# Local-attention stack: sums of squares behind the rope products, seeds ahead of the copy of O, band mask as eight tiled matmuls

## The reference

```
q, k, v = split(shift_tokens(x) @ Wqkv)          # 16 heads of 64
q = q / max(|q|, 1e-12) * q_scale;  k likewise   # one norm per token and head
q = q*cos*scale + rotate_half(q)*sin*scale;  k with 1/scale
# windows of 32 queries; each sees its own and the previous window, 64 keys
sim = einsum(q, keys) * 8
sim = where((i < j) | (i > j + 32) | (j is before the sequence), -max, sim)
out = softmax(sim) @ values;   x = out @ Wo + x
```

## Time and profile before

| what | us |
|---|---|
| median of 3 runs | 4362.58 (4357.62 to 4364.63) |
| the profiled execution's own time | 4365.13 |
| its span | 4363.3 |
| PE busy / weight loads | 3866.2 / 2314.4 |
| DVE / ACT / POOL busy | 3296.5 / 2534.1 / 2498.8 |

### The profile page before, as it was taken

One profiled execution on the slowest core, in us unless ns is written; L12 is line 12 of the kernel. 1 busy time (PEld: TensorE's weight loads), 2 busy tenths in 40 slices (PEclk: granted clock), 3 DMA queues, 4 the chain that ended last, 5 costly groups with the idle time before them and its releaser, 6 DMA issues. The chain is left out here.

```text
span 4363.3 us, 151598 instructions
## 1 busy us (share of the span) xinstructions
PE 3866.2 (89%) x66488; PEld 2314.4 (53%) x66488; DVE 3296.5 (76%) x4385; ACT 2534.1 (58%) x3236; POOL 2498.8 (57%) x2036
## 2 busy tenths in 40 slices
PE   6887799999999999999778877899999999999997
PEld 3323456665665666665433334566666666666664
DVE  7997777888888787888454436788888878878884
ACT  6885456566665666666324444556566565666654
POOL 0001677777777777777100005786777777777773
PEclk8999999999999999999789998999999999999998
DMA  0001232332323233222000002323323223232221
GB/s 19 1 1 42 72 87 65 85 77 75 83 67 87 73 78 85 62 67 62 17 1 1 1 14 74 92 62 84 81 67 85 73 79 80 73 81 71 66 60 40
DMA packets 165593, 260.83 MB, mean 60 GB/s; under 512 B 58572, under 2 KB 79816, under 8 KB 164936
## 3 DMA queue, kind: packets, MB, share of 16 engines
q1 hardware_dynamic: 164936, 251.13, 22.2%
HBM read 48.61 MB, written 1.05 MB: 11 GB/s over the span
## 5 line engine op out<-in xcount | busy, mean ns | idle before, releaser
L1374 POOL TENSOR_TENSOR f_k_rotated<-f_rope_ak,f_rope_bk 128x1024 f32<-128x1024 f32 x192 | 454.5, 2367 | 288.7 <-DVE f_rope_bk L1429 288.7
L1097 PE MATMUL banks<-f_wqkv,H 128*128 128x512 f32 x1152 | 564.9, 614 | 17.4 <-DVE f_E L1469 9.2
L1097 PE MATMUL banks<-f_wqkv,G 128*128 128x512 f32 x1152 | 551.8, 601 | 0.0
L1426 DVE TENSOR_TENSOR f_rope_aq<-banks,f_rope 128x1024 f32<-128x1024 f32 x192 | 235.1, 1225 | 389.5 <-ACT f_sqq L1284 376.2
L1361 POOL MEMSET f_kT<- 128x256 f32 x2 | 0.6, 311 | 839.9 <-POOLq L514 460.5
L1374 POOL TENSOR_TENSOR f_q_rotated<-f_rope_aq,f_rope_bq 128x1024 f32<-128x1024 f32 x192 | 454.5, 2367 | 29.0 <-DVE f_rope_bq L1429 28.6
L1319 ACT ACTIVATE f_V<-banks 128x1024 f32<-128x1024 f32 x192 | 196.8, 1025 | 418.7 <-PE banks L1097 418.3
L1152 PEld LDWEIGHTS banks<-f_O_T,f_wo 128*128 128x128 f32 x3072 | 372.6, 192 | 98.3 <-issue 94.6
L1152 PE MATMUL banks<-f_O_T,f_wo 128*128 128x128 f32 x3072 | 375.4, 275 | 6.4 <-issue 5.2
L1392 POOL TENSOR_TENSOR f_E<-f_E,f_row_inverse 128x1024 f32<-128x1024 f32 x192 | 368.6, 1920 | 19.8 <-DVE f_row_inverse L1484 19.8
L1386 POOL TENSOR_TENSOR f_q_rotated<-f_q_rotated,f_inverse_norm 128x1024 f32<-128x1024 f32 x192 | 365.2, 1902 | 15.0
(11 more groups left out here) (207 smaller groups left out, 8961.6 us busy)
## 6 DMA issues: line engine op xcount, KB each, us to landing
f_P_T_paired<-f_P_T SPq DMA_DIRECT2D x1536, 64.0 KB
f_V_previous<-f_V SPq DMA_DIRECT2D x192, 384.0 KB, 3.7
f_V_previous<-f_V SPq DMA_DIRECT2D x192, 128.0 KB, 2.4
f_wqkv<-in_L_ffn_Wqkv SPq DMA_DIRECT2D x48, 384.0 KB, 4.1
f_rope<-in_rope SPq DMA_DIRECT2D x24, 512.0 KB, 5.1
f_wo<-in_L_ffn_Wo SPq DMA_DIRECT2D x12, 512.0 KB, 5.4
f_w<-in_L_ffn_W SPq DMA_DIRECT2D x12, 341.0 KB
f_w<-in_L_ffn_W SPq DMA_DIRECT2D x24, 64.0 KB
```

What stands on the lines that cost most here:

```text
L1097: mm = nc.tensor.matmul(ps[:, o * BLK:(o + 1) * BLK], xs, w[:, c * INNER + o * BLK:c * INNER + (o + 1) * BLK], start=True, stop=True)
L1374: nc.gpsimd.tensor_tensor(qk[i][:], ra[i][:], rb[i][:], ALU.add).then_inc(radd.sem, 1)
L1426: nc.vector.tensor_tensor(heads_of(ra[i][:]), src, table(2 * i, 0, DH), ALU.mult).then_inc(rot.sem, 1)
```

## The change

Three edits in the stack. On DVE the sum of squares of q follows directly behind the rope products of q, and the sum for k and the clamp directly behind those of k. On ACT the Ln and Exp of the seeds stand ahead of the copy of O. On PE the mask is written by eight matmuls of 64 rows and 32 columns, in the tiling of the score matmuls, in place of two of 128 by 128; for this the mask table has one more block of entries set.

```
@@ scores
-                for i in range(2):
-                    nc.tensor.matmul(PT_S[:, i * BLK:(i + 1) * BLK], ident16[:],
-                                     mask[:, (1 if t else 0):(2 if t else 1), :].to_broadcast([P, HP, 2 * W]),
-                                     start=True, stop=False)
+                for g in range(NG):
+                    v = 1 if t or g else 0
+                    for i in range(2):
+                        rows = slice(i * DH, (i + 1) * DH)
+                        nc.tensor.matmul(PT_S[g * W:(g + 1) * W, i * BLK:(i + 1) * BLK], ident16[rows, i * DH:i * DH + W],
+                                         mask[rows, v:v + 1, :].to_broadcast([DH, HP, 2 * W]), start=True, stop=False)
@@ scalar
+                if live(s):
+                    act.wait_ge(clamped.sem, clamped.at(n))
+                    act.wait_ge(newton.sem, newton.past(n - 1))
+                    nc.scalar.activation(lg[:], ss[n % 2][:], ACT.Ln).then_inc(seeded.sem, 1)
+                    act.wait_ge(seeded.sem, seeded.at(n, 1))
+                    nc.scalar.activation(y0[:], lg[:], ACT.Exp, scale=-0.5).then_inc(seeded.sem, 1)
                 if live(s - 3):
                     act.wait_ge(o_mm.sem, o_mm.at(n - 3))
...
-                if live(s):
-                    act.wait_ge(clamped.sem, clamped.at(n))
-                    act.wait_ge(newton.sem, newton.past(n - 1))
-                    nc.scalar.activation(lg[:], ss[n % 2][:], ACT.Ln).then_inc(seeded.sem, 1)
-                    act.wait_ge(seeded.sem, seeded.at(n, 1))
-                    nc.scalar.activation(y0[:], lg[:], ACT.Exp, scale=-0.5).then_inc(seeded.sem, 1)
@@ vector
                     rotate(s, 0, q_mm, PQ)
+                    sums(n, 0)
...
                     rotate(s, 1, k_mm, PK)
+                    sums(n, 1)
+                    dve.wait_ge(red.sem, red.at(n))
+                    nc.vector.tensor_scalar(ss[n % 2][:], ss[n % 2][:], 1e-24, None, ALU.max).then_inc(clamped.sem, 1)
...
-                if live(s):
-                    sums(n, 0)
-                    sums(n, 1)
-                    dve.wait_ge(red.sem, red.at(n))
-                    nc.vector.tensor_scalar(ss[n % 2][:], ss[n % 2][:], 1e-24, None, ALU.max).then_inc(clamped.sem, 1)
@@ constants
     band[0:W, 0, 0:W] = NEG
+    band[2 * W:3 * W, 0, 0:W] = NEG
```

## The result

The changed kernel takes 4792.62 us (median of 4 runs, 4787.78 to 4800.77) against 4363.6 before: a ratio of 1.0988 (1.0969 to 1.1007), 429 us slower. The forecast was 4396 with a range of 4352 to 4430. The sign was right, the size was wrong: 34 us forecast, 429 measured.

The account below looks back on a forecast made before the run. A ring of waits through k's normalisation, not PE, was taken to pace the slot; the change makes the subtraction's ring bind. 4365.1 + 49 - 15 = 4399, on the median 4396 us; range 4352 to 4430.

Parts of the forecast that it names:

- The ring through the norms: k transposes to normalised k, through DVE, ACT and POOL: paces the old slot, loses 3.5 us, no longer binds.
- the ring through the subtraction: From q's projection through DVE's subtraction to PE's wait and the next projection: binds at 17.46 us in most slots.
- The length of the new ring: 18.56 + 17.46 + 17.46 + 16.60 = 70.08 us per group against 68.96: +1.12, over 44 groups +49 us.
- The first slots, -15 us: Slots without feed-forward work: new ring 16.60 or less against 17.54 a slot, about -15 us over two calls.
- Sum k to clamp 1.24, clamp 0.09: DVE terms of the new ring, ahead of the maximum (1.25) and the subtraction (1.22), in us.
- The clock: Rival: PE's new idle time costs clock; called unlikely. Shares the much slower case's chance of 0.10 with serial masks.
- the 2.35 of the earlier trace: PE's idle time in us in an early slot, where granted clock was 0.89; new waits were expected shorter.
- The mask: Eight mask matmuls on PE: 0.38 us for 0.52, gain 0.14 a slot, invisible because PE waits anyway.
- the lower bound of 0.26: Mask matmuls on PE if all eight tiles run together as one stream: 0.26 us.
- 4.6: How many score matmuls run abreast in the same tiling; used to price the eight masks at 0.38 us.
- ACT: Seeds ahead of the copy of O: delay it at most about half a us, no effect on time.

Follow-up runs that it names:

- the late clamp: Changed kernel with the clamp moved behind the subtraction and the seeds in their old place on ACT: 4394.93 us, ratio 1.0071.
- the two runs with the clock up: Changed kernel without the clamp, 4381.76 us; changed kernel with three useless matmuls on PE ahead of the wait for the subtraction, 4633.25 us.
- the filled wait: Changed kernel with three useless 512-column matmuls on PE ahead of the wait for the subtraction: 4633.25 us, ratio 1.0624.
- two other runs: ACT edit alone on the kernel before, 4784.04 us; changed kernel with the clamp behind the subtraction, seeds ahead of the copy of O, 4637.1 us.

## Why the prediction was right and wrong

- **The ring through the norms goes, the ring through the subtraction takes over**: right. The waits for POOL at L1229 and L1235 fell to 5 and 0 us, the wait for f_E rose to 343.5.
- **The length of the new ring**: right but for one term. It was added up as 70.08 us for a group of four slots, with 1.33 us from sum k through the clamp to the maximum. Without the clamp that is 1.12, thus 70.08 - 4 x 0.21 = 69.24; measured without the clamp, 4 x 17.35 = 69.4.
- **The first slots, -15 us**: too much. From the first to the ninth start of the products of q it is 134.0 us in the kernel before and 131.0 without the clamp, thus 3 us a call, 6 in all; the forecast went by the clamps, whose ninth already stands in a slot with feed-forward work. That the kernel without the clamp (18 us slower than before) and the late clamp (30) lie near the forecast +34 is in part luck: with 69.24 for a group its sum would have been 0.28 x 44 - 15 = -3 us.

```profile
L1426 DVE TENSOR_TENSOR f_rope_aq<-banks,f_rope x9: 1224/1225/1225, 418.5 to 552.5; 128x1024 f32<-128x1024 f32 x9
L1428 DVE TENSOR_TENSOR f_rope_aq<-banks,f_rope x9: 1224/1225/1225, 417.3 to 548.3; 128x1024 f32<-128x1024 f32 x9
```

- **"Sum k to clamp 1.24, clamp 0.09"**: this is the step that failed. The clamp was priced from its old place, with POOL idle beside it, and carried to one where POOL's addition of k is under way. It measured 1.23 us (1120.26 to the maximum at 1121.49) for the forecast 0.09: 1.14 x 192 = 219 us over the forecast, or 257 by the rows and 251 by the two runs with the clock up, if the kernel without a clamp is the measure. The prediction went through what each engine's queue holds behind a moved instruction, but not through what runs on the other engines beside it in its new place. "SBUF — State Buffer" of the Trainium skill (Who interferes with whom) states the rule: DVE and GpSimd share a pair of SBUF ports, which one instruction holds to its end; a tensor_scalar can need them, a tensor_reduce does not, and a DVE instruction with two SBUF inputs does against a GpSimd instruction that reads. All three agree with the rows here (1.31 us and 0.22 us beside the same addition; f_xn).
- **The clock**: the rival was named, priced at next to nothing and dismissed because the new waits were taken to be 1.2 to 2 us. With the blocked clamp PE's wait in the slot shown is 2.66 us, above the 2.35 of the earlier trace rows that the argument rested on, and at least 159 us went with the clock, as the filled wait shows. The reasoning held for the waits it was made for: without the clamp the granted clock of the steady stretch is 1.00.
- **In sizes**: 18 us for the rings with the longer f_xn, about 251 for the clamp, about 159 for the clock. These are differences between four kernels in a row and add up to 429 by themselves; what checks them is that the second is near the 257 of the rows.
- **The mask**: its eight matmuls start within 0.02 us and the scores 0.2 us later, under the forecast 0.38 and even under the lower bound of 0.26. All eight ran abreast, where the prediction went by 4.6. Worth nothing while PE waits (mask alone), 20 us once it nearly doesn't: right.

The mask matmuls and the first scores of the changed kernel:

```profile
1114.31 0.41 PE L1108 MATMUL banks<-f_band_mask,ident 64*32 64x512 bf16 x8
1114.53 0.69 PE L1116 MATMUL banks<-f_kT,f_qT 64*32 64x64 f32 x49
```

- **ACT**: "nothing" was wrong in its size: the whole change is 65 us slower than the DVE edit alone, and the mask's matmuls got shorter. The granted clocks (0.93 against 0.950 to 0.965) would fit with PE's idle time gathered in one wait; no run isolates that. That the ACT edit is dear without the DVE edit was right.

## What to carry to other kernels

Price a moved instruction by what runs on the other engines beside its new place, not by its duration in the old one. Here a DVE tensor_scalar of 128 x 32 numbers, from SBUF to SBUF, lasted until the GpSimd instruction beside it ended, and a tensor_reduce in its stead did not. Look at the longest instance of a line as well as the median: 289 ns beside 180 was the sign. Where two rings of waits have nearly the same length, move only as much as evens them out; the sum of q alone was worth -1.3%, the whole change +10%. A longer wait of PE can cost most of its length again through the clock behind it: here 1.34 us a slot of blocked clamp, and at least 0.8 (159/192) for the clock.

## What was not expected of the hardware

A DVE instruction on 32 numbers a row took 1300 to 1327 ns in all 192 slots and ended 0.03 to 0.04 us behind POOL's. An instruction of 0.71 us with two SBUF inputs (f_xn) took 1.2 us in the change, 1.8 without the clamp and 2.2 in two other runs, and in the slot shown POOL's next one took 2.36 us instead of 1.92. And 2.6 us of useless matmuls per slot made a kernel 159 us faster.
